# A banded attention layer between two feed-forward layers: the product with the values is put four units behind the scores, and the transposition of x one unit later

## The chip, the cores and the metric

The kernel runs on one core of one Trainium2 chip. The metric is the device time of one execution in microseconds (us). The engines are named as in the profile: PE (TensorE, matrix products; PEld are its weight loads), DVE (VectorE), ACT (ScalarE), POOL (GpSimd), and SP (SyncE), which here only issues DMAs.

## The reference

The input is x of 4 sequences x 2048 tokens x 256 features. Three layers follow each other, each added to x: half a feed-forward layer with ternary weights (256 to 1024 to 256), an attention layer, and the same half feed-forward layer again. The attention, cut to what matters here (16 heads of 64, blocks of 128 tokens):

```
q, k, v = x @ Wq / 8, x @ Wk, x @ Wv                  # after a layer norm
side_k, side_v = the same of the sums of 16 tokens    # 128 further keys per sequence
k_cat = [block n-1, block n, block n+1, side]         # 512 keys for the 128 queries of block n
probs = softmax with one extra logit of 0 (q k_cat^T + band mask)
y = probs @ v_cat;  x = x + y @ Wo
```

## The kernel before

The feed-forward phases (about the first 340 us and the last 260 us) are not touched. The attention phase has 64 blocks of 128 queries, 16 heads each, so 1024 heads `v`. There is no scheduler: every engine runs its own hand-written stream, and all streams walk through the same **units** `u`, one for each head (`j, h = divmod(u, 16)`; below "unit 5" is h = 5 of a block). In unit `u` an engine works on a head that is some units ahead of or behind `u`; semaphore counts hold the streams together.

- PE, `body` under `@block.tensor`: in every fourth unit the scores of four heads at once (`scores`, L1122 and L1125, heads u+4 to u+7); in every unit a piece of an *item* (`block_item`, taken from the table `PIECES`), and the product of one head with the values (`values`, L1147).
- DVE: `largest` takes the mask and the maximum of head u+4 (L1354); `split_high` (L1366, every fourth head, in units 1, 5, 9, 13) rounds head u+2 to its high half; `low` (L1346) makes an item's low half.
- ACT: `high` (L1263) makes an item's high half, `split_high` (L1302) rounds head u+2 (the other three of four), `exponentials` (L1286) handles head u+3.
- POOL: `split_low` (L1013) makes the low half of head u+2. SP: `turn_probs` (L987) transposes the two halves of head u+1 by DMA into one of six buffers `probsT`; it waits for the low half, and for the product of head v-6 that read the buffer before.

`PV_LAG` says how many units the product with the values runs behind the unit: in unit u it takes head u-3.

The items of a block are, in order: V1, Q0 (units 2 and 3), XTR, Q1, YT1, K0, OUTP, K1, YT0, V0. XTR (`turn_x`, L1080) transposes the normalised x of a later block on PE; YT1 and YT0 (`turn_y`, L1087) transpose the two halves of y. An item that PE has finished in one unit is copied by ACT and DVE in the next (`due`). On DVE the copies of that kind come before `largest` in units 0, 4, 8, 12, and after it in the others.

PSUM bank `y_ps1` is shared: heads 8 to 15 of a block are summed in it, then DVE divides it by the denominators (`invert_denominators`, L1402, and `normalise_y`, L1408), and only then may XTR write into it. XTR therefore waits for `y_done` of the second half of the block before:

```
                if kind == XTR:
                    y_done.wait(pe, at.halves + 2 * j - 1)
                    turn_x(bank, at.blocks + j + 2)
```

Of the kernel before, what the change touches and what calls it, by code (L numbers as in the profile page):

```python
# [697 lines left out]
def attention_phase(nc, w):  # L698
# [23 lines left out]
    V1, Q0, XTR, Q1, YT1, K0, OUTP, K1, YT0, V0 = PLAIN = range(10)  # L722
# [5 lines left out]
    SIDE_LAST, RIGHT_FIRST, OWN_FIRST = ORDERS = ((LEFT, OWN, RIGHT, SIDE_TILE), (RIGHT, LEFT, OWN, SIDE_TILE),  # L728
                                                  (OWN, RIGHT, LEFT, SIDE_TILE))
    MASK_OF = {SIDE_LAST: 0, RIGHT_FIRST: 4, OWN_FIRST: 3}  # L730
    PIECES = [[(V1, 0)], [(V1, 1)], [(Q0, 0)], [(Q0, 1)], [(XTR, 0), (Q1, 0)], [(Q1, 1)], [(OUTP, 0)], [(OUTP, 1), (YT1, 0)],
              [(K0, 0)], [(K0, 1)], [(OUTP, 2)], [(OUTP, 3)], [(K1, 0)], [(K1, 1)],
              [(YT0, 0), (V0, 0)], [(V0, 1)]]
    XTR_SLOT = 4
    FIRST_SIDE = {0: SK1, 5: SV1}
    LAST_SIDE = {10: SK0, 15: SV0}
    TURNS = (XTR, YT1, YT0)
# [6 lines left out]
    U = RING * H  # L744
    ROUNDS = BLK_PER_BATCH // RING
    STATS_SLOT, NORM_SLOT = 6, 14
    SCORE_AHEAD, EXP_AHEAD, SPLIT_AHEAD, TURN_AHEAD, PV_LAG = 4, 3, 2, 1, 3
    NBUF = 4
    NPARTS = 6
    CLEARED = 4  # L750
# [8 lines left out]
    with ExitStack() as ctx:  # L759
# [127 lines left out]
        def side_item(at, j, h):  # L887

            if at.first and j == 0:
                return FIRST_SIDE.get(h)  # L890
            if at.last and j == RING - 1:
                return LAST_SIDE.get(h)
            return None

        def finished(at, j, h):

            side = side_item(at, j, h)
            return [(j, k) for k, piece in PIECES[h] if piece == N_PIECES[k] - 1] + ([(j, side)] if side else [])

# [21 lines left out]
        def place_of(at, v):  # L921

            j = v // H
            if (at.first and j == 0) or (at.last and j == RING):
                return FIRST
            if (at.last and j == RING - 1) or (at.first and j < 0) or isinstance(at, End):
                return LAST
            return INNER
# [38 lines left out]
        def turn_count(at, v):  # L967

            return ((at.heads + v) // NPARTS + 1) * 16

        def started(at, v):

            return at.heads + v >= 0

        def ring(at, v):
            return (at.heads + v) % NPARTS

        def half(v):
            return (v % H) // (H // 2)
# [68 lines left out]
        def _(pe):  # L1048
# [9 lines left out]
            def bank_free(index, gap):  # L1058
                pe.wait_ge(lo_done, index - (gap - 1))
# [72 lines left out]
            def values(at, v):  # L1132

                j, h = divmod(v, H)
                if h == 0:
                    pe.wait_ge(lo_done, at.before(j))
                if h == H // 2:
                    pe.wait_ge(lo_done, at.item(j, YT1) + 1)
                if not started(at, v):
                    pe.sem_inc(pv_done.sem, 1)  # L1140
                    return
                pe.wait_ge(turned[ring(at, v)], turn_count(at, v))
                out = y_ps[half(v)][:, (h % 8) * DH:(h % 8 + 1) * DH]
                low = 4 if place_of(at, v) == INNER else 3
                passes = [(t, slot, a, b) for t, slot in tiles_of(at, v) for a, b in ((HI, HI), (HI, LO), (LO, HI))]
                for n, (t, slot, a, b) in enumerate(passes):
                    last = nc.tensor.matmul(out, pt[ring(at, v)][:, low * a + t, :],  # L1147
                                            vr[:, slot, b, h * DH:(h + 1) * DH],
                                            start=(n == 0), stop=(n == len(passes) - 1))
                last.then_inc(pv_done.sem, 1)  # L1150

            def side_source(b):
                return lambda k, s: w.g[:, k, s, bass.ts(b, P)]

            def block_item(at, b, j, kind, pieces):
                index = at.item(j, kind)
                bank, gap = at.place(j, kind)
# [3 lines that stand above are left out]
                    return  # L1161
                if kind == YT0:
                    turn_y(0, at.halves + 2 * j)
                    return
                if kind == YT1:
                    pe.wait_ge(lo_done, at.item(j, XTR) + 1)
                    turn_y(1, at.halves + 2 * j - 1)
                    return
                if 0 in pieces:
                    bank_free(index, gap)  # L1170
                if kind == OUTP:
                    project_out(bank, at.item(j, YT1), pieces)
                elif kind in (SK0, SV0):
                    project(kind, bank, side_source(b + 1), pieces)
                elif kind in (SK1, SV1):
                    project(kind, bank, side_source(b), pieces)
                else:
                    if kind == K0 and 0 in pieces:
                        pe.wait_ge(lo_done, at.item(j, XTR) + 1)
                    project(kind, bank, block_source(j if kind in (K0, K1, V0) else j + 1), pieces)  # L1180
# [17 lines left out]
            def body(at, b):  # L1198
                for u in range(U):
                    j, h = divmod(u, H)  # L1200
                    if u % NBUF == 0:
                        for pair in range(0, NBUF, 2):
                            scores(at, u + SCORE_AHEAD + pair)
                    side = side_item(at, j, h)
                    if side == SK1:
                        block_item(at, b, j, side, (0, 1))
                    for kind, piece in PIECES[h]:
                        if kind not in TURNS:
                            block_item(at, b, j, kind, (piece,))
                    if h == XTR_SLOT:  # L1210
                        block_item(at, b, j, XTR, (0,))
                    if side in (SK0, SV0, SV1):
                        block_item(at, b, j, side, (0, 1))
                    values(at, u - PV_LAG)
                    for kind, piece in PIECES[h]:
                        if kind in (YT0, YT1):
                            block_item(at, b, j, kind, (piece,))
# [3 lines left out]
            pe.wait_ge(lo_done, PRE_ITEMS)  # L1221
            batches(pe, body)
            end = End()
            values(end, -3)
            values(end, -2)
            values(end, -1)
# [103 lines left out]
        def _(dve):  # L1330
# [69 lines left out]
            def invert_denominators(at, v):  # L1400
                denom_done.wait(dve, at.halves + 2 * (v // H) + half(v))
                mark(nc.vector.reciprocal(rden[:], denom[:]))  # L1402

            def normalise_y(at, v, items_before):
                step_done()
                pv_done.wait(dve, at.heads + v)
                dve.wait_ge(item_done, items_before)
                nc.vector.tensor_tensor(y[:].rearrange("p (h e) -> p h e", h=8),  # L1408
                                        y_ps[half(v)][:].rearrange("p (h e) -> p h e", h=8),
                                        rden[:].unsqueeze(2).broadcast_to([P, 8, DH]),  # L1410
                                        ALU.mult).then_inc(y_done.sem, 1)
# [25 lines left out]
            def body(at, b):  # L1437
                count["base"], count["n"] = at.round * PER_ROUND + before, 0
                for u in range(U):
                    j, h = divmod(u, H)  # L1440
                    if u % NBUF:
                        split_high(at, u + SPLIT_AHEAD)
                        largest(at, u + SCORE_AHEAD)
                    for n, kind in due(at, u):
                        item(at, n, kind)
                    if u % NBUF == 0:
                        split_high(at, u + SPLIT_AHEAD)
                        largest(at, u + SCORE_AHEAD)
                    if h == STATS_SLOT:
                        moments(at.blocks + j + 3)  # L1450
                    if h == STATS_SLOT + 1:
                        mean_variance()
                        add_eps()
                    if h == NORM_SLOT:
                        normalise_x(at.blocks + j + 3, at.item(j, XTR) + 1)
                    if h in (2, 10):
                        invert_denominators(at, u - 3)
                    if h in (3, 11):
                        normalise_y(at, u - 4, at.before(j) if h == 3 else at.item(j, YT1) + 1)
                    for n, kind in due_late(at, u):  # L1460
                        item(at, n, kind)
                assert count["n"] == PER_ROUND

            batches(dve, body)
            end = End()
# [34 lines left out]
```

## Time and profile before

| | us |
|---|---|
| median of 3 runs (lowest, highest) | 2184.44 (2178.49, 2189.72) |
| profiled execution, its own time | 2183.18 |
| its span, first to last instruction | 2181.5 |
| attention phase (first to last product with the values) | 340.6 to 1920.0, so 1579.4 |
| one unit of it, on average (1024 units) | 1.542 |

The 1.7 us between span and time lie outside the program's instructions. A busy share is not a share of what an engine could do; idle time of an engine matters only where another engine waits for it.

### The profile page before, as it was taken

The numbers are of one execution on the slowest core, as the hardware profiler recorded it, in microseconds if no ns is written. First come the engines' busy times: TensorE is split into PE (matmuls) and PEld (weight loads), VectorE is DVE, ScalarE is ACT, GpSimd is POOL, SyncE is SP. The second block draws the span as 40 slices with busy tenths as digits, with TensorE's granted clock in tenths as the row PEclk, the third lists the DMA queues.
The fourth block names the chain that finished last, engine by engine and source line by source line (L and its number), as shares of the span: only waits on it lengthen the run. The fifth ranks groups of instructions, "written<-read, shape, count | busy, mean of one in ns | idle before, by whom it ended". The sixth has DMA issues, their size and how long they took to land. (4 is left out here: it accounts for less than half of the span.)

```text
span 2181.5 us, 77479 instructions
## 1 busy us (share of the span) xinstructions
PE 2049.6 (94%) x30286; PEld 1567.5 (72%) x30286; DVE 1879.6 (86%) x4646; ACT 1930.1 (88%) x4210; POOL 1406.1 (64%) x1455
## 2 busy tenths in 40 slices
PE   5999979999999999999999999999999999979999
PEld 3666657777777777777777778777777777746666
DVE  7999968889998898898979899998889889867776
ACT  5899958999999899999989999998999999969997
POOL 2444536777787687777767777786777777722221
PEclk9999989999999999999999999999999999989999
DMA  7888837999999899999989999999999999958998
GB/s 210 154 156 153 158 61 124 172 166 176 171 173 171 132 174 170 172 178 168 171 143 162 172 174 169 178 179 152 149 171 172 169 177 175 163 87 177 179 179 182
DMA packets 1341581, 355.54 MB, mean 163 GB/s; under 512 B 1321760, under 2 KB 1340192, under 8 KB 1341216
## 3 DMA queue, kind: packets, MB, share of 16 engines
q1 hardware_dynamic: 1341216, 350.59, 100.4%
q8 instruction: 239, 3.92, 0.7%
q14 instruction: 126, 1.03, 0.2%
HBM read 14.68 MB, written 8.39 MB: 11 GB/s over the span
## 5 line engine op out<-in xcount | busy, mean ns | idle before, releaser
L1013 POOL TENSOR_TENSOR probs_split<-probs,probs_split 128x512 f16<-128x512 f32 (+1 forms) x1026 | 1159.3, 1130 | 385.3 <-ACT probs_split L1302 281.3
L1286 ACT ACTIVATE probs<-probs,minus_max 128x512 f32<-128x512 f32 (+1 forms) x1027 | 717.0, 698 | 27.1 <-DVE minus_max L1354 26.9
L1354 DVE CUSTOM_DVE_ANT_0 probs<-score_ps,mask,neg_qk_scale 128x512 f32<-128x512 f32 (+1 forms) x1028 | 723.5, 716 | 9.6 <-PE score_ps L1125 8.3
L1147 PEld LDWEIGHTS y_ps<-v_parts,probsT 128*128 128x128 f16 x11904 | 457.7, 98 | 149.4 <-DMA probsT<-probs_split 71.1
L1147 PE MATMUL y_ps<-v_parts,probsT 128*128 128x64 f16 x11904 | 514.8, 193 | 51.4 <-DMA probsT<-probs_split 49.8
L1302 ACT ACTIVATE probs_split<-probs 128x512 f16<-128x512 f32 (+1 forms) x770 | 470.2, 611 | 8.5 <-DMA probsT<-probs_split 0.3
L1122 PE MATMUL score_ps<-k_parts,q_parts 64*128 64x384 f16 (+3 forms) x2604 | 371.1, 286 | 4.7 <-DVE k_parts L1346 2.7
L1125 PE MATMUL score_ps<-k_parts,q_parts 64*128 64x384 f16 (+3 forms) x2604 | 371.1, 286 | 0.0
L1122 PEld LDWEIGHTS score_ps<-k_parts,q_parts 64*128 64x128 f16 x2604 | 200.5, 94 | 108.0 <-issue 13.2
L1054 PE MATMUL item_ps<-b_xT,wk_split 128*128 128x128 f16 x3168 | 221.7, 220 | 1.9 <-DVE v_parts L1346 1.5
L1054 PE MATMUL item_ps<-wo_split,yT_parts 128*128 128x256 f16 x1560 | 213.9, 274 | 6.1 <-DVE v_parts L1346 4.6
L1054 PE MATMUL item_ps<-b_xT,wq_split 128*128 128x128 f16 x3120 | 218.2, 220 | 1.2 <-DVE b_xT L1346 0.9
L1054 PE MATMUL item_ps<-wv_split,b_xT 128*128 128x512 f16 x786 | 212.3, 380 | 0.0
L1054 PEld LDWEIGHTS item_ps<-b_xT,wk_split 128*128 128x128 f16 x3168 | 180.3, 98 | 35.7 <-issue 22.1
L1366 DVE CAST probs_split<-probs 128x512 f16<-128x512 f32 (+1 forms) x256 | 181.0, 707 | 27.8 <-ACT probs L1286 27.7
L1125 PEld LDWEIGHTS score_ps<-k_parts,q_parts 64*128 64x128 f16 x2604 | 200.4, 94 | 0.0
L1286 ACT ACTIVATION_READ_ACCUMULATOR probs<-probs,minus_max 128x1 f32 x1027 | 194.2, 189 | 0.0
L1054 PEld LDWEIGHTS item_ps<-b_xT,wq_split 128*128 128x128 f16 x3120 | 178.6, 98 | 18.7 <-issue 12.9
L1054 PEld LDWEIGHTS item_ps<-wo_split,yT_parts 128*128 128x128 f16 x1560 | 135.7, 98 | 19.5 <-DVE v_parts L1346 5.1
L1346 DVE TENSOR_TENSOR yT_parts<-y_ps,yT_parts 128x512 f16<-128x512 f32 x129 | 88.5, 686 | 54.4 <-ACT yT_parts L1263 54.3
L1346 DVE TENSOR_TENSOR v_parts<-item_ps,v_parts 128x512 f16<-128x512 f32 x140 | 95.7, 686 | 43.5 <-ACT v_parts L1263 43.4
L1263 ACT ACTIVATE k_parts<-item_ps 128x512 f16<-128x512 f32 x141 | 84.2, 597 | 53.8 <-PE item_ps L1054 51.5
(172 smaller groups left out, 3452.1 us busy)
## 6 DMA issues: line engine op xcount, KB each, us to landing
probsT<-probs_split SPq DMA_TRANSPOSE x1025, 3.9
out_x<-x_resident SPq DMA_DIRECT2D x64, 128.0 KB, 2.0
x_resident<-in_L_attn_x SPq DMA_DIRECT2D x56, 128.0 KB, 2.7
h_a<-in_L_ffn_w_up SPq DMA_DIRECT2D x1, 1024.0 KB, 5.8
scratch_a<-in_L_ffn_w_down SPq DMA_DIRECT2D x1, 1024.0 KB, 8.0
x_resident<-in_L_attn_x SPq DMA_DIRECT2D x2, 512.0 KB, 9.4
raw_q_a<-in_L_attn_Wq SPq DMA_DIRECT2D x1, 1024.0 KB, 11.5
raw_k_a<-in_L_attn_Wk SPq DMA_DIRECT2D x1, 1024.0 KB, 11.8
```

Source lines behind the costliest of these rows:

```text
L1013: nc.gpsimd.tensor_tensor(parts_of[ring(at, v)][:, LO, low_columns(place_of(at, v))], probs[v % NBUF][:, cols], parts_of[ring(at, v)][:, H ...
L1054: last = nc.tensor.matmul(out, left(k, a), right(k, b), start=(k == 0 and m == 0), stop=(k == n - 1 and m == 2))
L1122: even = nc.tensor.matmul(score_ps[v % NBUF][:, t * P:(t + n) * P], qs[0:DH, j % 2, q_part, cols], kr[0:DH, slot:slot + n, k_part, cols], ...
L1125: odd = nc.tensor.matmul(score_ps[v % NBUF + 1][:, t * P:(t + n) * P], qs[DH:P, j % 2, q_part, cols], kr[DH:P, slot:slot + n, k_part, cols ...
L1147: last = nc.tensor.matmul(out, pt[ring(at, v)][:, low * a + t, :], vr[:, slot, b, h * DH:(h + 1) * DH], start=(n == 0), stop=(n == len(pas ...
L1263: nc.scalar.activation(dst, src, ACT.Copy).then_inc(hi_done, 1)
L1286: nc.scalar.activation(probs[v % NBUF][:, cols], probs[v % NBUF][:, cols], ACT.Exp, bias=bias[:, j % 2, h:h + 1], scale=-1.0, accum_out=su ...
L1302: nc.scalar.activation(parts_of[ring(at, v)][:, HI, cols], probs[v % NBUF][:, cols], ACT.Copy).then_inc(phi_done[v % 4], 1)
L1346: nc.vector.tensor_tensor(dst, src, hi, ALU.subtract).then_inc(lo_done, 1)
L1354: nc.vector.tensor_tensor_reduce(out=probs[v % NBUF][:, cols], in0=score_ps[v % NBUF][:, cols], in1=mask_of(at, v), scale=w.neg_qk_scale[: ...
L1366: nc.vector.tensor_copy(parts_of[ring(at, v)][:, HI, cols], probs[v % NBUF][:, cols]).then_inc(phi_done[v % 4], 1)
```

## The change

The product with the values takes head u-4 in unit u (`PV_LAG` 4, and one more product after the last unit). What follows the end of a half of y moves one unit on as well: the reciprocal from units 2 and 10 to 3 and 11, the division by it from units 3 and 11 to 4 and 12. XTR moves from unit 4, where it stood behind the first piece of Q1, to unit 5, where it stands ahead of the second piece of Q1.

```diff
-    PIECES = [[(V1, 0)], [(V1, 1)], [(Q0, 0)], [(Q0, 1)], [(XTR, 0), (Q1, 0)], [(Q1, 1)], [(OUTP, 0)], [(OUTP, 1), (YT1, 0)],
+    PIECES = [[(V1, 0)], [(V1, 1)], [(Q0, 0)], [(Q0, 1)], [(Q1, 0)], [(XTR, 0), (Q1, 1)], [(OUTP, 0)], [(OUTP, 1), (YT1, 0)],
...
-    XTR_SLOT = 4
+    XTR_SLOT = 5
...
-    SCORE_AHEAD, EXP_AHEAD, SPLIT_AHEAD, TURN_AHEAD, PV_LAG = 4, 3, 2, 1, 3
+    SCORE_AHEAD, EXP_AHEAD, SPLIT_AHEAD, TURN_AHEAD, PV_LAG = 4, 3, 2, 1, 4
...
+                    if h == XTR_SLOT:
+                        block_item(at, b, j, XTR, (0,))
                     for kind, piece in PIECES[h]:
                         if kind not in TURNS:
                             block_item(at, b, j, kind, (piece,))
-                    if h == XTR_SLOT:
-                        block_item(at, b, j, XTR, (0,))
...
             end = End()
+            values(end, -4)
             values(end, -3)
...
-                    if h in (2, 10):
-                        invert_denominators(at, u - 3)
                     if h in (3, 11):
-                        normalise_y(at, u - 4, at.before(j) if h == 3 else at.item(j, YT1) + 1)
+                        invert_denominators(at, u - 4)
+                    if h in (4, 12):
+                        normalise_y(at, u - 5, at.before(j) if h == 4 else at.item(j, YT1) + 1)
```

PE, an inner block, from the end of the scores of unit 4 to the end of unit 7. Before:

```order
L1125 MATMUL score_ps<-k_parts,q_parts 128x384
L1054 MATMUL item_ps<-b_xT,wq_split 128x128 x12
L1080 MATMUL y_ps<-ident,b_x_normed 128x128 x2
L1147 MATMUL y_ps<-v_parts,probsT 128x64 x12
L1054 MATMUL item_ps<-b_xT,wq_split 128x128 x12
L1147 MATMUL y_ps<-v_parts,probsT 128x64 x12
L1054 MATMUL item_ps<-wo_split,yT_parts 128x256 x6
```

The same place after the change:

```order
L1125 MATMUL score_ps<-k_parts,q_parts 128x384
L1054 MATMUL item_ps<-b_xT,wq_split 128x128 x12
L1147 MATMUL y_ps<-v_parts,probsT 128x64 x12
L1080 MATMUL y_ps<-ident,b_x_normed 128x128 x2
L1054 MATMUL item_ps<-b_xT,wq_split 128x128 x12
L1147 MATMUL y_ps<-v_parts,probsT 128x64 x12
L1054 MATMUL item_ps<-wo_split,yT_parts 128x256 x6
```

XTR (L1080) has changed places with one product with the values (L1147), and nothing else on PE has moved; that product is of head 0 of the block now as it was of head 1 before.

DVE, the same inner block, units 2 to 6. `ISA` is `largest` and its read of the maximum; q_parts is the low half of Q0, and further down of Q1; lines from L1346 on carry numbers higher by one after the change. Before:

```order
L1346 TENSOR_TENSOR v_parts<-item_ps,v_parts 128x512
L1402 RECIPROCAL inv_denominator<-denominator 128x8
L1354 ISA probs,minus_max<-score_ps,mask,neg_qk_scale 128x512
L1354 ISA minus_max 128x1
L1408 TENSOR_TENSOR y<-y_ps,inv_denominator 128x512
L1346 TENSOR_TENSOR q_parts<-item_ps,q_parts 128x512
L1354 ISA probs,minus_max<-score_ps,mask,neg_qk_scale 128x512
L1354 ISA minus_max 128x1
L1366 CAST probs_split<-probs 128x512
```

After the change:

```order
L1347 TENSOR_TENSOR v_parts<-item_ps,v_parts 128x512
L1355 ISA probs,minus_max<-score_ps,mask,neg_qk_scale 128x512
L1355 ISA minus_max 128x1
L1403 RECIPROCAL inv_denominator<-denominator 128x8
L1347 TENSOR_TENSOR q_parts<-item_ps,q_parts 128x512
L1355 ISA probs,minus_max<-score_ps,mask,neg_qk_scale 128x512
L1355 ISA minus_max 128x1
L1409 TENSOR_TENSOR y<-y_ps,inv_denominator 128x512
L1367 CAST probs_split<-probs 128x512
```

The division into y stood ahead of the low half of Q0 and of `largest` of head 8; now it stands behind both. The streams of SP are the same in both kernels; ACT copies XTR in unit 6, ahead of Q1, where it did so in unit 5.

## Rows read from the trace of the kernel before

**Rows 1.** The page: busy time, PE and its granted clock in 40 slices.

```profile
PE 2049.6 (94%) x30286; PEld 1567.5 (72%) x30286; DVE 1879.6 (86%) x4646; ACT 1930.1 (88%) x4210; POOL 1406.1 (64%) x1455
...
PE   5999979999999999999999999999999999979999
...
PEclk9999989999999999999999999999999999989999
```

**Rows 2.** Busy time in the attention phase alone (stretch, length, engines, clock, DMA).

```profile
340.60:1920.00 1579.40, 1519.79 (x26341) 1204.28 (x26338) 1399.05 (x3463) 1450.03 (x3528) 1210.71 (x1214) 1.00 1.10 167
```

**Rows 3.** Waits of PE and PEld for the DMA: total, times, longest; then L1147's group.

```profile
PE y_ps L1147 <- DMA probsT<-probs_split: 49.8, 88, 1.5
...
PEld y_ps L1147 <- DMA probsT<-probs_split: 71.1, 124, 1.7
...
L1147 PE MATMUL y_ps<-v_parts,probsT 128*128 128x64 f16 x11904 | 514.8, 193 | 51.4 <-DMA probsT<-probs_split 49.8
```

**Rows 4.** Timeline of PE at the first and the last late product (start, length, idle before).

```profile
369.13 0.82 PE L1054 MATMUL item_ps<-wo_split,yT_parts 128*128 128x256 f16 x6
369.84 0.52 PE L1147 MATMUL y_ps<-v_parts,probsT 128*128 128x64 f16 x12
...
1902.06 0.82 PE L1054 MATMUL item_ps<-wo_split,yT_parts 128*128 128x256 f16 x6
1904.34 0.43 PE L1147 MATMUL y_ps<-v_parts,probsT 128*128 128x64 f16 x9 [1.46 <-DMA probsT<-probs_split]
```

**Rows 5.** PE, an undisturbed inner block: YT0 (L1087), then Q0, Q1, XTR.

```profile
1250.58 0.64 PE L1087 MATMUL y_ps<-ident,y 128*128 128x128 f32 x4
...
1256.59 0.83 PE L1054 MATMUL item_ps<-b_xT,wq_split 128*128 128x128 f16 x12
1257.26 0.51 PE L1147 MATMUL y_ps<-v_parts,probsT 128*128 128x64 f16 x12
1259.12 0.84 PE L1054 MATMUL item_ps<-b_xT,wq_split 128*128 128x128 f16 x12
1259.80 0.39 PE L1080 MATMUL y_ps<-ident,b_x_normed 128*128 128x128 f32 x2
1260.03 0.51 PE L1147 MATMUL y_ps<-v_parts,probsT 128*128 128x64 f16 x12
1260.38 0.83 PE L1054 MATMUL item_ps<-b_xT,wq_split 128*128 128x128 f16 x12
```

**Rows 6.** ACT in the same block: high halves of YT0 and Q0.

```profile
1251.26 0.60 ACT L1263 ACTIVATE yT_parts<-y_ps 128x512 f16<-128x512 f32 x1
...
1258.78 0.58 ACT L1263 ACTIVATE q_parts<-item_ps 128x512 f16<-128x512 f32 x1
```

**Rows 7.** DVE in the same block, units 3 to 5.

```profile
1258.20 0.68 DVE L1408 TENSOR_TENSOR y<-y_ps,inv_denominator 128x512 f32<-128x512 f32 x1
1259.39 0.69 DVE L1346 TENSOR_TENSOR q_parts<-item_ps,q_parts 128x512 f16<-128x512 f32 x1 [0.51 <-ACT q_parts L1263]
1260.00 0.74 DVE L1354 CUSTOM_DVE_ANT_0 probs<-score_ps,mask,neg_qk_scale 128x512 f32<-128x512 f32 x1
...
1260.66 0.73 DVE L1366 CAST probs_split<-probs 128x512 f16<-128x512 f32 x1
```

**Rows 8.** First and last block: DVE behind `largest` of head 8, PE's XTR.

```profile
343.58 0.45 DVE L1366 CAST probs_split<-probs 128x384 f16<-128x384 f32 x1
...
342.74 0.39 PE L1080 MATMUL y_ps<-ident,b_x_normed 128*128 128x128 f32 x2
...
1900.08 0.45 DVE L1366 CAST probs_split<-probs 128x384 f16<-128x384 f32 x1
...
1899.73 0.39 PE L1080 MATMUL y_ps<-ident,b_x_normed 128*128 128x128 f32 x2
```

**Rows 9.** The transposes: length on SP min/median/max in ns, time to landing in us.

```profile
L987 SPq DMA_TRANSPOSE probsT<-probs_split x1025: 1209/1287/2722, 327.3 to 1917.4; - x171
...
DMA to landing us min/median/max: 2.7/3.9/6.0
```

**Rows 10.** A unit with scores: PE's product in unit 0, POOL's low half.

```profile
1254.22 0.51 PE L1147 MATMUL y_ps<-v_parts,probsT 128*128 128x64 f16 x12
...
1254.16 1.16 POOL L1013 TENSOR_TENSOR probs_split<-probs,probs_split 128x512 f16<-128x512 f32 x1 [0.55 <-ACT probs_split L1302]
```

## Prediction

> **What bounds the kernel now.** The granted clock of PE is at or near its upper level (2.4 GHz) in all but two of the 40 slices, and in the attention phase it is 1.00 [rows 1, 2]. In that phase PE is busy 1519.8 of 1579.4 us, ACT 1450.0, DVE 1399.1 [rows 2]. PE sets the pace, so what counts is what PE waits for. There the table of waits names one thing: the product with the values, L1147, waits for the transposed probabilities, 49.8 us on PE and 71.1 us on PEld [rows 3]. All idle time ahead of L1147 is 51.4 us, of 59.6 that PE idles in the phase (1579.4 - 1519.8).
>
> The 51.4 is too little. A group's modelled end lies past the start of the next: 0.51 us long, and the next starts 0.35 later [rows 5]. So I took the lost time from starts. A product normally starts 0.65 to 0.67 us after its item's piece. At the last late one that is 2.28 us, 1.63 lost where 1.46 of idle is shown; at the first it is 0.71, 0.06 lost and none shown [rows 4]. Over 149 late products it adds up to 73.1 us, 1.14 a block, close to PEld's 71.1.
>
> By unit, 57 of them (31.4 us) lie in units 14, 15 and 0 to 3, and 92 (41.8 us) in units 4 to 13. This split decides the forecast.
>
> **The change, part by part.**
>
> *Four units behind instead of three.* PE's work is the same, a product only stands one unit later. A unit without scores takes PE 1.02 us (1256.59 from its item's piece to the next unit's scores, 0.67 + 0.35), one with scores 2.8 (1257.26 to 1260.03) [rows 5]. So a transpose gets at least 1.02 us more. The longest wait is 1.5 us, and 17 of the 149 lose over 1 us; 13 of these are in units 3, 7 and 11, which get the 2.8. I take it that all 73.1 us of waiting go; up to 3 us may stay.
>
> What this costs on SP: transposing head v waits for the product of head v-6, which now comes one unit later, in unit v-2. In the worst place, a unit with scores, that product stands at 1254.22 and is over at 1254.73, and the low half for which the same transpose waits is over at 1254.16 + 1.16 = 1255.32 [rows 10]. The low half is still last. Zero; if it turned, the new slack of 1.02 us would cover it first.
>
> *The division one unit later, and XTR behind it.* Here a wait is added. XTR may write `y_ps1` only when DVE has divided it. In the undisturbed block [rows 5 to 7]:
> - Before, the division starts at 1258.20 and ends at 1258.88; XTR comes at 1259.80, 0.92 later. It never waits.
> - After, the division stands behind the low half of Q0 (start 1259.39) and `largest` of head 8 (1260.00). It starts where the cast now starts, 1260.66, takes 0.68, and signals at about 1261.38 (0.04 for the semaphore, my estimate from 1259.39, which is 0.03 past the end of ACT's 1258.78 + 0.58).
> - Taking the division out of unit 3 does not bring the low half of Q0 forward: DVE idles 0.51 us before it, until ACT has made the high half [rows 7]. The reciprocal falls into the same idle time.
> - PE is there earlier. The product takes XTR's old place, 1259.80, and XTR could start 0.35 later, at 1260.15.
> - XTR waits 1261.38 - 1260.15 = **1.23 us**. Behind it on PE stand the second piece of Q1 and everything else.
>
> The same sum for each of the 64 blocks (start after `largest` of head 8, plus 0.72, minus XTR's old start, minus 0.35, or 0.26 in blocks with three tiles) is positive in 59, mean 0.88, sum **56.3 us**. The first block gives 343.58 + 0.72 - 342.74 - 0.26 = 1.30, the last 1900.08 + 0.72 - 1899.73 - 0.26 = 0.81 [rows 8]. Blocks without a late product in units 14 to 3 give nearly always 1.23 or 1.26; those with one give less by about the time lost.
>
> That is the point. ACT starts on YT0 0.04 us after PE has finished it (1250.58 + 0.64, 1251.26 in rows 5 and 6), and from there ACT runs almost without a gap to the high half of Q0 at 1258.78, then DVE to the division. This stretch from YT0's end to the division's signal takes 10.2 us (1251.22 to 1261.38), whatever PE waits for meanwhile. PE's own work up to XTR takes 8.9 (1251.22 to 1260.15). So in units 14 to 3 the removed DMA waits buy nothing: they turn into a longer wait at XTR. The 56.3 us hold against PE as it runs before, with its 31.4 us of such waits; these stay in the sum. Only the waits in units 4 to 13 are gained.
>
> *Later on DVE.* The cast of head 7 and `largest` of heads 9 to 11 start 0.68 later. XTR's low half, behind `largest` of head 10, is then done some 2.3 us after XTR's start (0.66 + 0.66 + 0.66 + 0.34), and YT1, which waits for it, comes after 3.3 (XTR 0.23, three pieces with three products at 1.02). Zero, with 1 us to spare. For the second half the division goes to unit 12, and its reader YT0 stands in unit 14: zero. The further product at the end is the one that the first unit no longer has.
>
> **Sum:** 2183.18 (profiled execution) + 56.3 - 41.8 = 2197.7; I forecast **2198 us**. The profiled execution is 1.3 us below the median of 2184.44, inside the runs' spread of 11 us. "Faster" and "slower" mean by over 0.5% (11 us), about what a measurement of this kernel can tell from no change: below 2173.5 or above 2195.4. The forecast is only just on the slow side.
>
> **The rivals.**
>
> *A. XTR hardly waits, the DMA waits go.* 2183.2 - 73.1 = 2110 with no wait, 2138 with half of it. For it: DVE has 180 us of idle time in the phase, and a stream with less behind it may come earlier. Against: the low half of Q0 waits for ACT, not for DVE's own work, and ACT's chain starts at PE's YT0. Chance 0.07.
>
> *B. Both sums hold in full.* If the chain to the division were anchored later than YT0, say at the scores of unit 4, the waits of units 14 to 3 would be gained as well: 2183.2 + 56.3 - 73.1 = 2166, faster by 0.8%. It decides at how much of the 31.4 us comes back: with over 24 the kernel is faster. Against: blocks with such waits show a smaller difference at XTR. Chance 0.13.
>
> *C. The waits stay, since SP's queue is full.* A transpose holds SP 1.287 us of a unit of 1.542, 84% of the phase of 1579.4 (1025 transposes) [rows 9]. Were SP the limit, one more unit of distance would be used up once and PE would wait as before: 2183.2 + 56.3 = 2239. Against: a queue that needs 1.29 us a unit doesn't limit units of 1.54; the late ones are those at the end of a burst of short units of 1.02. Chance 0.06. The Trainium skill, "Perfetto Trace Analysis", section "What 'DMA-bound' means", has the rule behind this: a kernel is bound on the DMA sequencer where the issuing engine's track is solid DMA slices. By that rule the longer distance brings nothing; the trace, at 84%, comes near to it but doesn't reach it.
>
> *D. XTR's wait drags more with it.* The second pair of scores in unit 8 waits for `largest` of head 11, which I put at 3.9 us after XTR's start, against PE's 4.4 there. Should it be late by 0.3 in each block, that is 19 us: 2217. Chance 0.07.
>
> **How the numbers follow.** The forecast has 0.67; its own range is 2186 to 2210: three quarters of the waits in units 4 to 13 gained (+10), or another 10 us of small waits behind XTR gone. Of it, about 0.42 lies above 2195.4 and 0.25 within. Slower: 0.42 + 0.06 + 0.07 = 0.55. Within: 0.25 + 0.02 of B = 0.27. Faster: 0.07 + 0.11 = 0.18. The range 2166 to 2220 leaves out A, C, and half of B.
>
> **What the next profile would show.** (1) The wait of L1147 for the DMA falls from 71.1 us on PEld to under 5; if it stays above 30, C. (2) A new wait, XTR (L1080) for DVE's y L1408, about 60 times, longest near 1.3 us, if PE had kept its old delays; since it also takes up the DMA waits of units 14 to 3, its total is near 56 + 31 = 88 us, some 1.3 us in nearly every block. Under 60 us is for B or A. (3) YT0's end to XTR takes 10.2 us in inner blocks. (4) ACT idles before the high half of XTR. What would make it wrong is above all an anchor of the chain that is not YT0.

## The result and the profile after

The changed kernel takes 2191.59 us (median of 6 runs, 2189.49 to 2198.28), the kernel before 2180.3 in the same comparison (6 runs, 2176.8 to 2189.72). The ratio is 1.0051, with a 95% interval of 1.0027 to 1.0076: slower by about 11 us, where 14 were forecast. The profiled execution took 2190.8 us, its span 2189.1.

The waits of PE and PEld in the changed kernel (total, times, longest), and L1147's group, against [rows 3]:

```profile
PE y_ps L1080 <- DVE y L1409: 69.4, 64, 1.4
...
PE y_ps L1147 <- DMA probsT<-probs_split: 1.3, 3, 0.6
...
PEld y_ps L1080 <- DVE y L1409: 77.1, 64, 1.5
...
PEld y_ps L1147 <- DMA probsT<-probs_split: 3.3, 9, 0.8
...
L1147 PE MATMUL y_ps<-v_parts,probsT 128*128 128x64 f16 x11904 | 513.6, 193 | 1.5 <-DMA probsT<-probs_split 1.3
```

Here `...` in a fence of waits stands for rows left out. The exchange is the one foretold: the wait for the DMA has gone from 71.1 us to 3.3 on PEld, and XTR (L1080) waits for the division in every one of the 64 blocks. By starts, the late products lose 2.9 us (10 of them) where they lost 73.1 (149), and XTR loses about 79.

The attention phase (stretch, length, busy time of PE, PEld, DVE, ACT, POOL), against [rows 2]:

```profile
340.80:1928.93 1588.13, 1508.83 (x26305) 1217.04 (x26302) 1374.81 (x3460) 1462.99 (x3522) 1209.01 (x1212) 1.00 1.10 166
```

It is 8.7 us longer (1588.1 against 1579.4), which is nearly all of what the span gained (2189.1 - 2181.5 = 7.6).

PE in an inner block of the changed kernel, from YT0 (L1087) to XTR, against [rows 5]:

```profile
1254.24 0.63 PE L1087 MATMUL y_ps<-ident,y 128*128 128x128 f32 x4
...
1262.78 0.84 PE L1054 MATMUL item_ps<-b_xT,wq_split 128*128 128x128 f16 x12
1263.46 0.51 PE L1147 MATMUL y_ps<-v_parts,probsT 128*128 128x64 f16 x12
1265.06 0.44 PE L1080 MATMUL y_ps<-ident,b_x_normed 128*128 128x128 f32 x2 [1.09 <-DVE y L1409]
```

DVE at the same place, against [rows 7]:

```profile
1263.05 0.69 DVE L1347 TENSOR_TENSOR q_parts<-item_ps,q_parts 128x512 f16<-128x512 f32 x1 [1.07 <-ACT q_parts L1264]
1263.66 0.74 DVE L1355 CUSTOM_DVE_ANT_0 probs<-score_ps,mask,neg_qk_scale 128x512 f32<-128x512 f32 x1
...
1264.32 0.69 DVE L1409 TENSOR_TENSOR y<-y_ps,inv_denominator 128x512 f32<-128x512 f32 x1
```

From YT0's end (1254.24 + 0.63 = 1254.87) to XTR are 10.19 us, where 10.2 were worked out from the trace of before. XTR could have started 0.35 after 1263.46, at 1263.81, and waits 1.25. Most blocks now look alike: from unit 15 to unit 15, 46 of 63 take 24.69 to 24.73 us, where before they took anything from 23.5 to 27.3.

So the signs that the prediction named are there (its total for XTR's wait, 88 us, came out as 79). That does not show that its sum is right: the two terms could be right in the trace and wrong in the time.

### The profile page after: what moved, and what is told of

Its sections match the earlier page's. It is cut to its first block and busy times, and to the rows that moved or that the text cites. A ratio compares the mean times of both kernels' runs of the same rounds, so it can differ in the third digit from the quotient of the medians.

```text
span 2189.1 us, 77480 instructions
## 1 busy us (share of the span) xinstructions
PE 2037.6 (93%) x30286; PEld 1580.1 (72%) x30286; DVE 1855.6 (85%) x4646; ACT 1944.9 (89%) x4210; POOL 1405.1 (64%) x1455
## 5 line engine op out<-in xcount | busy, mean ns | idle before, releaser
L1355 DVE CUSTOM_DVE_ANT_0 probs<-score_ps,mask,neg_qk_scale 128x512 f32<-128x512 f32 (+1 forms) x1028 | 726.3, 724 | 25.8 <-PE score_ps L1125 25.8
L1147 PE MATMUL y_ps<-v_parts,probsT 128*128 128x64 f16 x11904 | 513.6, 193 | 1.5 <-DMA probsT<-probs_split 1.3
L1147 PEld LDWEIGHTS y_ps<-v_parts,probsT 128*128 128x128 f16 x11904 | 464.6, 98 | 69.7 <-DMA probsT<-probs_split 3.3
L1122 PEld LDWEIGHTS score_ps<-k_parts,q_parts 64*128 64x128 f16 x2604 | 201.3, 94 | 106.2 <-issue 14.5
L1367 DVE CAST probs_split<-probs 128x512 f16<-128x512 f32 (+1 forms) x256 | 161.3, 630 | 7.9 <-ACT probs L1287 1.7
L1347 DVE TENSOR_TENSOR q_parts<-item_ps,q_parts 128x512 f16<-128x512 f32 x130 | 89.3, 687 | 76.6 <-ACT q_parts L1264 76.6
L355 DVE TENSOR_TENSOR h_split_c<-h_c,h_split_c 128x1024 f16<-128x1024 f32 x64 | 78.4, 1225 | 59.2 <-ACT h_split_c L660 58.0
```

Source lines behind the costliest of these rows:

```text
L1122: even = nc.tensor.matmul(score_ps[v % NBUF][:, t * P:(t + n) * P], qs[0:DH, j % 2, q_part, cols], kr[0:DH, slot:slot + n, k_part, cols], ...
L1347: nc.vector.tensor_tensor(dst, src, hi, ALU.subtract).then_inc(lo_done, 1)
L1355: nc.vector.tensor_tensor_reduce(out=probs[v % NBUF][:, cols], in0=score_ps[v % NBUF][:, cols], in1=mask_of(at, v), scale=w.neg_qk_scale[: ...
L1367: nc.vector.tensor_copy(parts_of[ring(at, v)][:, HI, cols], probs[v % NBUF][:, cols]).then_inc(phi_done[v % 4], 1)
```

## The experiments

All times are medians in us, the ratio is to the kernel before on the same chip, with its 95% interval. In the four kernels with fewer transposes one head in four is not transposed, so their output is not that of the reference; they serve only to find the cause.

| kernel | time | before | ratio |
|---|---|---|---|
| changed | 2191.59 | 2180.3 | 1.0051 (1.0027 to 1.0076) |
| lag alone | 2178.98 | 2181.88 | 0.9988 (0.9977 to 0.9999) |
| changed, division put back | 2180.01 | 2181.88 | 0.9994 (0.9982 to 1.0007) |
| moves alone, lag three | 2195.93 | 2181.88 | 1.0072 (1.0056 to 1.0089) |
| XTR alone moved | 2184.15 | 2181.88 | 1.0019 (1.0008 to 1.0029) |
| lag alone, fewer transposes | 2114.5 | 2182.58 | 0.9686 (0.967 to 0.9702) |
| changed, fewer transposes | 2188.14 | 2182.58 | 1.0025 (1.0015 to 1.0035) |
| before, more DMA issues | 2322.82 (one run) | 2182.58 | - |
| before, fewer transposes | 2116.54 | 2179.09 | 0.9706 (0.9681 to 0.9731) |
| moves alone, fewer transposes | 2188.94 | 2179.09 | 1.0046 (1.003 to 1.0062) |
| pairs | 2204.96 | 2182.58 | 1.0101 (1.0086 to 1.0116) |
| pairs, eight sources | 2163.27 | 2179.09 | 0.9924 (0.9898 to 0.9949) |
| the same, less to clear | 2161.03 | 2180.21 | 0.9909 (0.9872 to 0.9945) |

### The change taken apart

**The lag alone.** Against the kernel before:

```diff
-    SCORE_AHEAD, EXP_AHEAD, SPLIT_AHEAD, TURN_AHEAD, PV_LAG = 4, 3, 2, 1, 3
+    SCORE_AHEAD, EXP_AHEAD, SPLIT_AHEAD, TURN_AHEAD, PV_LAG = 4, 3, 2, 1, 4
...
+            values(end, -4)
```

> The lag of four units alone: the division into y stays in units 3 and 11, the reciprocal in 2 and 10, XTR in unit 4 as before the change. Theory (the change's cost is the division put behind largest of head 8): the DMA waits of L1147 go (under 5 us on PEld), XTR doesn't wait, and the time is that of the changed kernel less the 79 us lost at XTR, 2191.6 - 79 = 2113, between 2105 and 2125. Rival 1 (ACT's chain from YT0 on sets the pace, XTR's wait only shows it): the time comes back as waits elsewhere on PE, 2150 or more. Rival 2 (the division must move with the lag, since it now waits on DVE for a product of its own unit): DVE idles before L1408 by 0.5 us or more, and the time is above 2140.

It took 2178.98 us. The first theory falls: taking XTR's wait out of the changed kernel gives back 13 us, not 79. Waits on PEld, then on PE and on DVE:

```profile
PEld y_ps L1147 <- DMA probsT<-probs_split: 70.9, 113, 2.3
PEld item_ps L1054 <- issue: 40.4, 121, 0.4
PEld score_ps L1122 <- DVE minus_max L1355: 32.0, 91, 1.1
...
PE y_ps L1147 <- DMA probsT<-probs_split: 37.6, 72, 2.2
...
DVE probs_split L1367 <- DMA probsT<-probs_split: 23.7, 32, 1.9
```

PEld waits for the DMA as long as before the change, 70.9 us, though each transpose has a unit more, and the longest wait is even longer, 2.3 us. PE itself waits less, 37.6 us against 49.8 [rows 3]; from starts, as the prediction counted, the late products lose about 55 us where they lost 73. Part of the rest has only moved. DVE's cast of every fourth head now waits 23.7 us for the transpose that last read its source buffer, a row that the kernel before doesn't have, and behind DVE the scores on PE wait for the maximum (32.0 us on PEld, 6.5 before). A distance of one unit would have ended the waits if the transposes were late by a fixed latency. Instead they have become later: a low half that POOL has finished lies 2.35 us on average until its transpose is issued, where it lay 1.35 in the kernel before. This is what a full queue does: it falls behind until the six source buffers, all in use, stop it.

The second rival put on record (the division must move with the lag) can't be the reason why the time is 66 us above the theory's 2113: DVE idles only 18 us in all ahead of the division, and a kernel further down, with the division at this same place, takes 2114.5.

**The division put back.** In the changed kernel:

```diff
-                    if h in (3, 11):
-                        invert_denominators(at, u - 4)
-                    if h in (4, 12):
-                        normalise_y(at, u - 5, at.before(j) if h == 4 else at.item(j, YT1) + 1)
+                    if h in (2, 10):
+                        invert_denominators(at, u - 3)
+                    if h in (3, 11):
+                        normalise_y(at, u - 4, at.before(j) if h == 3 else at.item(j, YT1) + 1)
```

> The changed kernel with the division and the reciprocal put back to units 3 and 11, 2 and 10; lag four and XTR in unit 5 stay. Theory: as with the lag alone, 2105 to 2125, since XTR's own place costs nothing; XTR (L1080) has no wait for y. If XTR's place in unit 5 matters by itself, this one stands clear of the lag alone by more than 5 us.

2180.01 us. The time is not as expected, but the two kernels agree within 1.1 us, so with lag four XTR's own place costs nothing that can be told.

**The moves alone, with lag three.** The changed kernel with the first diff of this section taken back.

> The moves without the lag: product three units behind as before, the division in units 4 and 12, XTR in unit 5. Theory (the stretch from YT0 to XTR has a fixed length, DMA waits inside it cost nothing more): before plus 56, 2180.3 + 56 = 2236, between 2228 and 2246; the DMA waits of L1147 stay near 73 us, those of units 14 to 3 among them. Rival (the wait at XTR and the DMA waits add in full, the chain being anchored later): 2180.3 + 79 = 2259 or more.

2195.93 us, 14 above before: neither the 56 of the theory nor the 79 of its rival. On PE, from 340 to 1925 us:

```profile
PE y_ps L1080 <- DVE y L1408: 58.9, 61, 1.2
PE y_ps L1147 <- DMA probsT<-probs_split: 9.1, 17, 1.1
```

Here nothing was done for the transposes, and yet the wait for them falls from 49.8 us on PE to 9.1. The only new wait is that at XTR, so it is this wait that removes them: PE is slower by a little, and the queue keeps up.

**XTR alone moved.** PIECES and `XTR_SLOT` as in the change, nothing else.

> XTR alone moved to unit 5; lag three, division in units 3 and 11. Theory: no difference to before, 2180 +- 6, no wait of XTR for y. Rival (XTR's later place delays YT1 by its low half): slower by 10 us or more, PE waiting before L1087.

2184.15 us, 2.3 above before. The wait of L1147 for the DMA is 53.3 us on PE; YT1 doesn't wait more than before. The difference is small but clear of no change (ratio 1.0008 to 1.0029); its cause stays open.

### The queue of the transposes

A second theory: SP, which does nothing but issue the transposes, is the bound of the phase. The timeline of SP in the kernel before, four issues in a row (start and length):

```profile
1009.92 1.29 SPq L987 DMA_TRANSPOSE probsT<-probs_split  x1
...
1011.30 1.28 SPq L987 DMA_TRANSPOSE probsT<-probs_split  x1
...
1012.67 2.32 SPq L987 DMA_TRANSPOSE probsT<-probs_split  x1
...
1015.08 1.29 SPq L987 DMA_TRANSPOSE probsT<-probs_split  x1
```

The issues stand end to end, 0.09 us apart. The third is 1.04 us longer than its neighbours. Over all 1025 issues of the kernel before, the median is 1.287 us [rows 9], but the mean is 1.433: 202 are longer than 1.5 us. With the 0.092 us between two that is 1.525 us per head, where a unit takes 1.542; in all it is 1563 us of the 1592 from the first issue to the end of the last, 98%. A low half that POOL has finished lay 1.35 us on average until its transpose was issued, and in 91% of cases more than 0.4.

**Fewer transposes, with the lag.** In `turn_probs`, a plain copy of the same bytes takes the transpose's place for one head in four:

```diff
+                if v % 4 == 1:
+                    sp.dma_start(pt[ring(at, v)][:, turned_tiles(at, v)],
+                                 flat(at, v).rearrange("p (t n) -> p t n", n=P)).then_inc(turned[ring(at, v)], 16)
+                    return
```

> The lag of four alone, and every fourth head's transpose (256 of 1024) replaced by a plain DMA copy of the same bytes on the same queue, so the products of those heads take untransposed data: the output is not the reference's. Theory 2 (SP's queue of transposes sets the pace of the attention phase: mean issue 1.44 us plus a gap of 0.09 against a unit of 1.54): a plain copy holds SP about 0.58 us, 0.85 less, 0.21 per unit, so SP needs 1.32 us per unit and PE's own 1.47 becomes the bound: 2179 - 65 = about 2115, between 2105 and 2130; DMA waits of L1147 under 10 us. Rival (a chain through ACT and the division sets it, or the DMA engines' bytes, which stay): 2170 to 2182.

2114.5 us, as expected. The products and all else on PE, ACT and DVE are the same in number; only the issues differ (length in ns, min/median/max):

```profile
L991 SPq DMA_TRANSPOSE probsT<-probs_split x769: 1210/1280/2782, 326.6 to 1847.0; - x193
L988 SPq DMA_DIRECT2D probsT<-probs_split x256: 464/541/2032, 328.2 to 1842.7; - x128
```

The stretch of the attention phase:

```profile
341.98:1849.87 1507.89, 1499.12 (x26302) 1205.66 (x26299) 1385.92 (x3459) 1437.61 (x3522) 1207.94 (x1212) 1.00 1.01 175
```

PE is busy for all but 8.8 of 1507.9 us, and most inner blocks take about 23.5. This run alone can't tell SP's issues from the DMA engines' own work: the DMA share has fallen too, to 1.01 from 1.10 [rows 2]. The run with more issues, further down, tells the two apart.

**Fewer transposes, in the changed kernel.**

> The changed kernel with the same replacement of every fourth transpose by a plain copy (the output is not the reference's). Theory 2: nothing gained, 2190 +- 5, since the blocks of the changed kernel are held at 24.73 us by the wait of XTR for the division and no longer by SP; the wait at XTR stays near 69 us. Rival (the changed kernel is also held by SP's queue): it falls by 20 us or more.

2188.14 us, with XTR's wait as it was:

```profile
PE y_ps L1084 <- DVE y L1413: 69.2, 64, 1.4
```

Relieving SP, which gave the lag-alone kernel 3%, gives the changed kernel hardly anything: its ratio to before is 1.0025 where it was 1.0051. It is held by the other thing, the wait at XTR.

**More issues.** In SP's `body` of the kernel before:

```diff
+                    if u % 4 == 1:
+                        n = extra_issues[0]
+                        if n:
+                            sp.wait_ge(half_set, 1 + 16 * n)
+                        sp.dma_start(idle_row[:], w.ident16[0:1, :]).then_inc(half_set, 16)
+                        extra_issues[0] += 1
```

> The kernel before with one further small DMA (256 bytes, one row) issued by SP in every fourth unit, 256 in all, that nobody but SP waits for. Theory 2: each holds SP about 0.45 to 0.6 us, 115 to 150 us in all, of which at most 24 us find SP free: slower by 85 to 135 us, 2267 to 2317. Rival (SP has 16% to spare, as the median issue suggests, 0.25 us a unit): within 15 us of before.

2322.82 us, 140 more, a little above the range. The small DMAs:

```profile
L999 SPq DMA_DIRECT2D idle_row<-ident x256: 568/579/1905, 337.4 to 2051.6; - x128
```

256 x (0.579 + 0.092) = 172 us of further work for SP. SP was free 2% of its 1590 us, 27 us; 172 - 27 = 145. (By the small DMAs' mean, 0.62, it is 155; the mean of the transposes fell to 1.41 in turn, 24 us in all.) A queue with the room that the medians suggested would have swallowed them. Nor is it the DMA engines that are full: in the attention phase their share (next to last figure of the row) falls to 0.99, from 1.10 before, while the kernel gets slower.

```profile
340.00:2050.00 1710.00, 1539.76 (x26286) 1196.97 (x26283) 1402.93 (x3458) 1458.83 (x3520) 1207.06 (x1211) 1.00 0.99 154
```

**Fewer transposes with lag three, and with the moves alone.** The same edit in the kernel before, and in the moves-alone kernel.

> The kernel before (lag three) with every fourth transpose replaced by a plain copy (output not the reference's). Theory 2: the lag hardly matters once SP is relieved, since the transposes were late by SP's backlog: 2114 to 2125, DMA waits of L1147 under 15 us. Rival (the lag is worth something by itself, the DMA's latency being the cause of the waits): 2140 or more.

> The moves without the lag (division in units 4 and 12, XTR in unit 5, product three behind), with every fourth transpose replaced by a plain copy (output not the reference's). Theory 2: the stretch from YT0 to XTR holds the block at 24.73 us whatever SP does, 2186 to 2194; against the kernel before with the same replacement the moves then cost about 70 us, where on the kernel as it is they cost 14. Rival (part of the wait at XTR was SP's): under 2170.

2116.54 and 2188.94 us, both as expected. With SP relieved, PE waits at L1147 for the DMA for 0.5 us in the kernel with lag three, and the lag is worth nothing that can be told (2114.5 against 2116.54, on different chips; the ratios' intervals overlap). The moves cost 72 us there (2188.94 - 2116.54), against 14 on the kernel as it is. On PE, moves alone with fewer transposes:

```profile
PE y_ps L1084 <- DVE y L1412: 69.0, 64, 1.2
```

### A version that beats both

If SP is the bound, half the issues should help. Two heads' rows are put side by side, and one DMA turns both; POOL clears the buffers first, since a pair is always turned whole. Against the lag-alone kernel, the main places:

```diff
+        parts_two = [sb(f"probs_split{n}", [P, 2, 2, 4 * P], F16) for n in range(NPARTS // 2)]
+        pt_two = [sb(f"probsT{n}", [P, 2 * 2 * 4, P], F16) for n in range(NPARTS // 2)]
+        parts_of = [parts_two[n // 2][:, n % 2] for n in range(NPARTS)]
+        pt = [pt_two[n // 2][:, 8 * (n % 2):8 * (n % 2) + 8] for n in range(NPARTS)]
...
-                sp.dma_start_transpose(pt[ring(at, v)][:, turned_tiles(at, v)], flat(at, v)).then_inc(turned[ring(at, v)], 16)
+                two = ring(at, v) // 2
+                sp.dma_start_transpose(pt_two[two][:], parts_two[two][:].rearrange("p h s n -> p (h s n)")
+                                       ).then_inc(turned_two[two], 16)
...
-                for u in range(U):
+                for u in range(0, U, 2):
                     turn_probs(at, u + TURN_AHEAD)
```

> The lag of four alone, and the transposes issued in pairs: two heads' halves (2048 columns) in one DMA, 512 issues instead of 1024; the six buffers become three double ones; nothing is left out. Theory 2: if an issue of twice the size holds SP well under twice as long (from six to eight tiles the median rose only from 1.237 to 1.288 us), SP is no longer the bound, and the time falls toward PE's own work, 2115 to 2140. Rival: the issue takes twice as long, or the DMA's bytes are the limit: 2175 to 2200; or the even head of a pair lands too late, and L1147 waits for the DMA at every second head.

2204.96 us: slower. An issue takes 2.19 us in the median (2.33 in the mean, so 1.17 per head), and the landing 4.9 us:

```profile
L992 SPq DMA_TRANSPOSE probsT<-probs_split x512: 1315/2192/3809, 333.7 to 1937.8; - x171
...
DMA to landing us min/median/max: 4.2/4.9/6.7
```

SP is now used 77% of the time. But ACT waits for source buffers, which a pair holds longer:

```profile
ACT probs_split L1310 <- DMA probsT<-probs_split: 99.8, 122, 1.7
```

So the sources were made eight, with the room from three unused blocks behind x:

```diff
-FRONT, BEHIND = 1, 3
+FRONT, BEHIND = 1, 0
...
+    NSRC = 8
...
-                if started(at, v - NPARTS):
-                    act.wait_ge(turned[ring(at, v)], turn_count(at, v - NPARTS))
+                if started(at, v - NSRC):
+                    act.wait_ge(turned[ring(at, v - NSRC)], turn_count(at, v - NSRC))
```

> The paired transposes again (lag four, division in units 3 and 11), but with eight source buffers probs_split in place of six, so that ACT's and DVE's rounding of head v waits for the transpose of head v-8, not v-6; the six probsT stay. Nothing is left out. Theory: the 100 us that ACT waited for the DMA in the first paired kernel were what held it (an issue of 2.19 us per pair leaves SP free), so ACT's wait goes under 20 us and the time falls to 2115 to 2145. Rival: DMA latency of a pair (4.9 us) makes PE wait for the even heads, PEld more than 60 us at L1147: 2160 to 2190.

2163.27 us, 0.8% below the kernel before and the first real gain, but short of the 2115 to 2145. ACT's wait for the DMA is gone from the table. What is left is what the rival named, and the time lies in its range of 2160 to 2190:

```profile
PEld y_ps L1154 <- DMA probsT<-probs_split: 59.4, 87, 1.7
```

SP is now used 80% of the time. All 92 late products of this trace are of even heads (47 of 98 are in the lag-alone kernel). An even head is ready a unit before the odd one but is turned together with it, and a pair also lands later (5.1 us against 3.9). Which of the two makes it late, no run tells apart.

The last kernel clears only the columns that the first block leaves unwritten:

```diff
-                nc.gpsimd.memset(two[:], 0.0).then_inc(parts_cleared, 1)
+                nc.gpsimd.memset(two[:, :, 0, 0:P], 0.0).then_inc(parts_cleared, 1)
+                nc.gpsimd.memset(two[:, :, 1, 3 * P:4 * P], 0.0).then_inc(parts_cleared, 1)
```

> The paired transposes with eight source buffers again; POOL clears at the start of the attention phase only the 128 columns at each end of a head's row that the first block never writes, not the whole buffers. Theory: the first product with the values came at 347.9 us against 340.6 in the kernel before, and most of that is the clearing, so 3 to 7 us come back: 2156 to 2161. Rival (the later start is that of waiting for the second head of the pair): 2162 to 2165.

2161.03 us, on the border between the two expectations. The first product comes at 344.6 us instead of 347.9, so the mechanism is there, but the ratios (0.9909 and 0.9924) overlap in their intervals: whether it is faster stays open.

## Why the prediction was right about the time, and wrong about what held the kernel

**Right: the wait at XTR.** The chain from YT0 over ACT and DVE to the division has a fixed length of 10.2 us, and PE's own work up to XTR is 8.9. Both held to 0.03 us in the block shown. This fixes most inner blocks at 24.7 us, with lag three or four, with SP relieved or not. The rival that the chain is anchored later (B) is out.

**Right as an account of PE in the changed kernel.** Both terms can be checked from starts. The DMA waits went (2.9 us left of 73.1), and XTR lost about 79 where 56 + 31 = 88 were foretold: together about +9, and the phase is 8.7 longer. The difference between 79 and 88 is a mistake in the split of the waits. Of the 31.4 us in units 14, 15 and 0 to 3, 6.7 (10 products) lie in unit 14, whose product stands ahead of YT0. They come before the chain begins, so they too were gained. With them on the other side the prediction's sum is 56.3 - 41.8 - 6.7 = 7.8 instead of 14.5, next to the 8.7 measured in the phase.

**Wrong: what removes the DMA waits.** The prediction took "PE sets the pace" and "all 73.1 us of waiting go" as what one unit more brings. The lag alone leaves PEld waiting 70.9 us, and is worth 3 us (ratio 0.9988). The moves alone, without the lag, bring PE's wait down from 49.8 to 9.1. The wait at XTR removed them. That they went at all, and with them the forecast's nearness, was luck: XTR's wait happens to hold a block at 24.7 us, just above what SP's queue needs.

**Wrong: the two terms as prices.** +56.3 for the moves and -41.8 for the lag look like the worth of two separate edits. No kernel pays either: where SP is the bound, the moves cost 14 us; where PE is, 72, and the lag brings 3 us or nothing. The right reading is a largest, not a sum. Per inner block, PE's own work takes 23.5 us (measured with SP relieved), SP's queue 16 x 1.525 = 24.4 and somewhat more with its idle moments (before: 1579.4 / 64 = 24.7 a block over all), the chain through XTR 24.73. The change takes a kernel at the second to the third, which lies a little above.

**The step that failed** is in rival C: "a queue that needs 1.29 us a unit doesn't limit units of 1.54". The 84% was 1025 times the median. The mean issue is 11% longer, since every fifth or so is held for 0.2 to 1.4 us more, and 0.09 us between two belong to each. The true share is 98%. By the Trainium skill, "Perfetto Trace Analysis", section "What 'DMA-bound' means", a kernel is bound on the DMA sequencer where the issuing engine's track is solid DMA slices. This trace agrees: 98% is solid, and 256 small DMAs more made the kernel 140 us longer. What C got wrong in turn is the end of its sum, 2239: the waits did not stay on top of XTR's wait, since both take the same slack.

D did not come: in the changed kernel PE waits for `largest` (minus_max, L1355) 7.4 us on PEld, 33 times, against 6.5 and 27 times before.

## What to carry to other kernels

A wait for a DMA that is late by a queue's backlog is not cured by more distance: the queue falls back by the same distance (a low half lay 2.35 us instead of 1.35), and the waits come again, in part at another engine. Whether a queue is full is read from the sum of its issues and of the gaps between them, never from the median; the test is to relieve the queue, or to load it further. Before adding terms for one engine, work out what each other bound gives per block, and take the largest: a wait is only worth what lies between it and the next bound.

## What the runs showed of the hardware

- The issue of a DMA transpose holds SP for 1.24 us with six tiles of 128 x 128 (2 bytes), 1.29 with eight and 2.19 with sixteen (medians, the last in the first kernel with pairs); a plain copy of the same bytes 0.54, one of a single row of 256 bytes 0.58. With eight tiles it hardly depends on how full SP is: 1.29 with SP in use 98% of the time, 1.28 with 86% (lag alone, fewer transposes).
- Of the 202 issues over 1.5 us in the kernel before, 97% have a packet of 1 KB or more of the instruction queues starting within them or in the half microsecond ahead; of the others 23% have one. The long issues are also longer windows: stretches of their length laid at random have one in 43% of cases. That the fetching of instructions holds the issue is a conclusion from this coincidence, which no run tests. It is what the median hides: the long issues come about every fifth transpose.
